# Cross-attention and expert layer of a gated Flamingo block: two heads on two partition halves instead of stacked copies of K and Q

## The reference

```python
xn = layernorm(x)
q1, k1, v1 = xn @ Wq1, xn @ Wk1, xn @ Wv1           # 8 heads of 64
k2, v2 = ctx @ Wk2, ctx @ Wv2
k, v = concat([k1, k2]), concat([v1, v2])            # 768 keys
out = softmax(q1 @ k.T / 8) @ v                      # for each batch and head
x = x + tanh(g_xattn) * (out @ Wo + bo)
xf = layernorm(x)                                    # then a mixture of experts
combine = softmax over the 2 largest of (xf @ gate_w + gate_b), 0 for the rest
y = sum_e combine[:, e] * (gelu(xf @ w1[e] + b1[e]) @ w2[e] + b2[e])   # 8 experts of 512
x = x + tanh(g_ffn) * (y + gelu(xf @ ws1 + bs1) @ ws2 + bs2)           # a shared ninth
```

## Time and profile before

| | us |
|---|---|
| median of 3 runs (172.03 to 174.6) | 172.52 |
| the profiled execution's own time | 172.02 |
| its span, first to last instruction | 169.7 |
| PE busy | 139.7 |
| DVE busy | 131.2 |
| POOL busy | 126.8 |
| ACT busy | 109.6 |
| share of the chain that ended last: PE, DVE, POOL, ACT, DMA and SP's queue | 32%, 28%, 10%, 9%, 14% |

### The profile page before, as it was taken

One profiled execution on the slowest core, in us unless ns is written; L12 is line 12 of the kernel. 1 busy time (PEld: TensorE's weight loads), 2 busy tenths in 40 slices (PEclk: granted clock), 3 DMA queues, 4 the chain that ended last, 5 costly groups with the idle time before them and its releaser, 6 DMA issues.

```text
span 169.7 us, 4332 instructions
## 1 busy us (share of the span) xinstructions
PE 139.7 (82%) x1724; PEld 111.5 (66%) x1724; DVE 131.2 (77%) x255; ACT 109.6 (65%) x182; POOL 126.8 (75%) x90
## 2 busy tenths in 40 slices
PE   7789588558699989999998892979866995999953
PEld 4435234335478768787787792869856994999952
DVE  1779999667667868768869689989999889454691
ACT  3369583329969979899968998569523462555600
POOL 7609999919999999989777955596557585868750
PEclk9999999999999999999999999999996999999999
DMA  4598699990004800995000000340000000100000
GB/s 136 184 315 211 196 238 242 220 251 14 6 0 85 198 1 16 217 233 191 4 4 0 4 0 0 108 144 6 2 0 0 4 0 4 31 0 4 0 0 31
DMA packets 12925, 13.99 MB, mean 82 GB/s; under 512 B 1470, under 2 KB 9579, under 8 KB 12907
## 3 DMA queue, kind: packets, MB, share of 16 engines
q1 hardware_dynamic: 12906, 13.73, 30.4%
HBM read 7.18 MB, written 0.26 MB: 44 GB/s over the span
## 4 chain that ended last, share of the span: by engine, by line
PE 32%; DVE 28%; POOL 10%; ACT 9%; DMA 8%; SPq 6%; issue 5%; DVEq 0%; ACTq 0%
PE banks L906 5%; DVE kab L852 5%; PE banks L908 5%; PE banks L907 5%; POOL kab L549 4%; ACT kab L642 4%; DVE v_lo L720 3%; DMA kab<-k_nat 3%; DVE nmax L735 3%; PE banks L1006 3%; PE banks L1007 3%; PE banks L987 3%; DMA ring<-in_L_ffn_w_dram 3%; SPq L425 2%; DVE gtop L763 2%
## 5 line engine op out<-in xcount | busy, mean ns | idle before, releaser
L549 POOL TENSOR_TENSOR kab<-kab 128x1024 f16<-128x1024 f32 (+1 forms) x18 | 41.1, 2283 | 17.3 <-DVE kab L852 17.3
L521 POOL TENSOR_TENSOR p_lo<-prob,p_hi 128x768 f16<-128x768 f32 x31 | 50.3, 1642 | 3.1 <-ACT p_hi L606 2.6
L642 ACT ACTIVATE kab<-banks,b1T 128x256 f32<-128x256 f32 x72 | 28.2, 478 | 24.3 <-PE banks L908 15.9
L735 DVE TENSOR_REDUCE nmax<-banks 128x1 f32<-128x768 f32 x32 | 30.5, 954 | 12.5 <-PE banks L988 12.5
L598 ACT ACTIVATE prob<-banks 128x768 f32<-128x768 f32 x32 | 25.8, 805 | 9.1 <-PE banks L1007 8.1
L906 PE MATMUL banks<-wf,kab 128*128 128x128 f16 x144 | 26.2, 224 | 5.8 <-POOL kab L549 4.5
L606 ACT ACTIVATE p_hi<-prob 128x768 f16<-128x768 f32 x32 | 27.0, 843 | 1.0
L852 DVE CAST kab<-kab 128x1024 f16<-128x1024 f32 (+1 forms) x19 | 19.5, 1031 | 9.8 <-ACT kab L642 9.8
L908 PE MATMUL banks<-wf,kab 128*128 128x128 f16 x144 | 26.2, 224 | 0.0
L907 PE MATMUL banks<-wf,kab 128*128 128x128 f16 x144 | 26.2, 224 | 0.0
L1006 PE MATMUL banks<-qab,kab 128*128 128x256 f16 x96 | 23.0, 273 | 0.7 <-DVE qab L832 0.7
(11 more groups left out here) (144 smaller groups left out, 340.3 us busy)
## 6 DMA issues: line engine op xcount, KB each, us to landing
ring<-in_L_ffn_w_dram SPq DMA_DIRECT2D x16, 256.0 KB, 4.1
kab<-k_nat SPq DMA_DIRECT2D x4, 384.0 KB, 4.4
kab<-k_nat SPq DMA_DIRECT2D x6, 192.0 KB, 4.4
kab<-k_nat SPq DMA_DIRECT2D x2, 576.0 KB, 7.2
qab<-qo SPq DMA_DIRECT2D x2, 384.0 KB, 6.2
kab<-k_nat SPq DMA_DIRECT2D x2, 288.0 KB, 7.8
prob<-in_ctx_dram SPq DMA_DIRECT2D x2, 256.0 KB, 5.4
ring<-in_L_xattn_Wk_dram SPq DMA_DIRECT2D x2, 256.0 KB, 3.9
```

The costliest lines, as they stand in the source:

```text
L521: nc.gpsimd.tensor_tensor(p_lo[:, j % 3, dst, :], prob(j, g)[:, 0:n, :], p_hi[:, j % 3, dst, :], ALU.subtract).then_inc(pl_done, 1)
L549: nc.gpsimd.tensor_tensor(hid_lo[:, k % HB, cols], hid[:, k % 2, cols], hid_hi[:, k % HB, cols], ALU.subtract).then_inc(hl_done, 1)
L642: nc.scalar.activation(hid[:, k % 2, c * T1:(c + 1) * T1], span(2 * (k % 2), HC * T1)[:, c * T1:(c + 1) * T1], ACT.Gelu, bias=b1T[:, e * H ...
L735: nc.vector.tensor_reduce(nmax[:, i, q:q + 1], span(0, KEYS), AX_X, ALU.max, negate=True).then_inc(max_done, 1)
```

## The change

The stacking copies, `kab` and `qab` are gone. Matmuls read the two heads of a pair where the projections left them, partitions 0 to 63 and 64 to 127, and the two heads' matmuls alternate, each into a PSUM bank of its own. With 64 rows a score tile needs four matmuls for each head (high·high, low·high, high·low, shift) in place of two; the shift is a product of a constant row block and a tile that DVE writes over all partitions.

The unit is now two heads by two key tiles (128x1024), three units a pair, 24 in all (NU). Maxima are taken in three chunks a pair of 128x1024, then reduced once more. Only four items precede the steps. The others lie in the dictionary `LATE`, from step -4 to step 10. Each step of PE: `shift_row`, `scores(i)`, `max_chunk`, expert work, `values`, items, tail. The scores have one PSUM buffer up to unit 12 and two from unit 13. There are 3 buffers of exponentials and 7 of their halves. `ring` has 7 places, and its loads wait for no attention step. POOL does the splits of experts 1 and 2, the bias and WO between the units. The tails begin at steps 16 and 27, the experts at FFN0 = 24.

```diff
-RING = 4
+RING = 7
+KT2 = 2
+UPP = KT // KT2
+NPAIR = B * PAIRS
+NU = NPAIR * UPP
+RINGP = 7
+RINGE = 3
+CHUNK0 = -(UPP + 1)
+DOUBLE0 = 13
+FFN0 = NU
-TAIL0 = [HEADS + PV_LAG, NH + PV_LAG + 1]
+TAIL0 = [16, 27]
-FSPLIT0 = 15
+FSPLIT0 = FFN0 - EARLY
+def chunk_of(s):
+    p, c = divmod(s - CHUNK0, UPP)
+    return (p, c) if 0 <= p < NPAIR else None
+def shift_of(s):
+    p, r = divmod(s + 1, UPP)
+    return p if r == 0 and 0 <= p < NPAIR else None
+def values_of(s):
+    if s >= NU + 1:
+        return NH - 2 + s - (NU + 1) if s <= NU + 2 else None
+    p, r = divmod(s - (UPP + 2), UPP)
+    return 2 * p + r if p >= 0 and r < 2 and p < NPAIR - 1 else None
+PRE = [(("tc", 0), 0), (("tx", 0), 2), (("k", 0, 0), 4), (("q", 0), 6)]
+LATE = {
+    -4: [(("k", 0, 1), 2)],
+    -3: [(("q", 1), 7)],
+    -2: [(("v", 0, 0), 6), (("v", 0, 1), 4)],
+    -1: [(("v", 0, 2), 5)],
+    0: [(("k", 0, 2), 4), (("q", 2), 7)],
+    1: [(("v", 0, 3), 6), (("v", 0, 4), 7)],
...
+    10: [(("v", 1, 4), 7), (("v", 1, 5), 4)],
+}
+def score_buf(u):
+    return 0 if u < DOUBLE0 else (u - DOUBLE0 + 1) % 2
@@ gpsimd
+            for i in range(STEPS):
+                if 0 <= i - 1 < LO_LAST:
+                    prob_lo(i - 1)
+                if i == 2:
+                    early_hi(1)
+                if i == 3:
+                    early_scaled(1)
+                if i == 4:
+                    early_lo(1)
+                if i == 5:
+                    add_bias()
+                if i == 6:
+                    early_hi(2)
+                if i == 7:
+                    early_scaled(2)
+                if i == 8:
+                    early_lo(2)
+                if i == 10:
+                    split_by_pool(WO)
@@ scalar
+            def exp_unit(u):
+                act.wait_ge(score_ps, u + 1)
+                if u >= RINGE:
+                    act.wait_ge(pl_done, u - RINGE + 1)
...
+                if 0 <= i < NU:
+                    exp_unit(i)
+                for n in items[0:1]:
+                    item_of(n)
+                if 0 <= i < NU:
+                    make_hi(i)
+                for n in items[1:]:
+                    item_of(n)
...
-                    if k >= 2:
+                    if k < 2:
+                        act.wait_ge(pl_done, NU - 2 + k)
+                    else:
@@ vector
+            def part_max(p, c):
+                dve.wait_ge(max_ps, UPP * p + c + 1)
...
+                nc.vector.tensor_reduce(dst, src, AX_X, ALU.max).then_inc(part_done, 1)
+            def whole_max(p):
...
+            def shift_out(p):
+                dve.wait_ge(shift_ps, p + 1)
...
@@ tensor
+            def max_chunk(p, c):
...
+                if c == 0:
+                    pe.wait_ge(item_hi, items_ready(("k", b, pp), ("q", pp)))
+                    if p == 0:
+                        read_out(before(NI, [0, 1]))
+                    else:
+                        pe.wait_ge(shift_done, p)
+                else:
+                    pe.wait_ge(part_done, UPP * p + c)
...
+            def scores(u):
...
+                for n in range(KT2):
...
+                    for half in range(2):
+                        nc.tensor.matmul(dst[:, half, cols], k_of(p, half, 0, keys), q_of(p, half, 0, every),
+                                         start=True, stop=False)
+                    for half in range(2):
+                        nc.tensor.matmul(dst[:, half, cols], k_of(p, half, 1, keys), q_of(p, half, 0, every),
+                                         start=False, stop=False)
+                    for half in range(2):
+                        nc.tensor.matmul(dst[:, half, cols], k_of(p, half, 0, keys), q_of(p, half, 1, every),
+                                         start=False, stop=False)
...
+                    for half in range(2):
+                        rows = slice(DH * half, DH * half + DH)
+                        last = nc.tensor.matmul(dst[:, half, cols], ones_row[rows, :], shift[rows, p % 2, :],
+                                                start=False, stop=True)
```

562 lines of the change are left out of this document (236 added, 326 removed), and 8 rows, old and new, of the table LATE.

## The result

| | before | after |
|---|---|---|
| median, us | 173.56 (172.03 to 174.76, 4 runs) | 187.49 (184.69 to 188.35, 4 runs) |
| profiled execution, us | 172.02 | 188.35 |
| its span, us | 169.7 | 186.6 |

The ratio is 1.0736, its 95% interval 1.0486 to 1.0985. By the medians the kernel is slower by 14 us; the prediction had it 3 us faster. Executions of one kernel differ here by 3 to 6 us: the ratios compare the shorter ones of either kernel, and the profiled execution of the kernel after is the longest of its four.

What follows compares the result with a forecast made beforehand. POOL was taken to set the pace of attention. From the profiled 172.02 us, 1.1 came off for an earlier last low half and 1.5 in the experts, giving 169.4 us; range 163.5 to 177.

Steps and rivals of the forecast that it cites:

- The lead-in: Before attention: with the stacking copies gone, first exponential at 24 us against 37.8, POOL's first low half at 27.2 against 43.76.
- The 64-row matmuls: PE's scores and maxima: alternating pairs on disjoint partitions run beside each other, 0.12 us a pair (bounds 0.11 to 0.22).
- The slow rival: 64-row matmuls run one by one, 0.22 us a pair, and PE is the bound from step 0: 180.3 us, chance 0.16.
- The price of POOL's work: POOL in attention: 23 low halves of 1024 at 2.13 us plus splits, bias and powers, sum 68.75 us.
- Can the others keep it busy?: Attention: POOL clearly slowest up to step 10 (39 us against ACT's 35); 2 us of pauses, last low half at 98.0.
- The lockstep rival: PE's in-order waits pass between engines; a late attention unit costs 2.6 us, not 2.25, over 13 units: 174 us, chance 0.17.
- The switches of rows: PE changing between 64 and 128 rows, 48 times: 0 to 0.16 us each, taken as 0.05, inside the 2 us of pauses.
- gelu 0 starts 2.0 us after POOL's last low half: Start of the experts: PE waits for the combination weights, so gelu 0 follows by 2.0 us, where it was 1.2 before.
- The experts: From attention's end to the end of the span: same work, 0 to 3.4 us gained together, 1.5 taken.
- The prediction's first step: Kernel before: POOL, with 50.3 us of work in 55.4 us, sets the pace of attention.

Runs made afterwards that it cites:

- halves apart: The changed kernel with the four score matmuls of one head first, then the four of the other: 187.34 us, profiled execution 182.73 us.
- tail two steps later: The changed kernel with the tail of batch 0 two steps later (TAIL0[0] 18 in place of 16): 181.68 us, ratio 1.0452.
- maxima and tail: The changed kernel with a pair's maxima and shift one step sooner and the tail of batch 0 two steps later: 175.97 us.
- the division ahead of the items: DVE divides a head before the items' low halves: in every step of the changed kernel, 189.26 us; only in steps with items, in the three moves, 172.55 us.
- the three moves: The changed kernel with maxima a step sooner, batch 0's tail two steps later, and DVE's division before low halves in steps with items: 172.55 us, ratio 0.9946.
- the kernel kept warm: The changed kernel with matmuls on zeros into an unread bank in three of PE's long waits: 184.82 us, profiled execution 183.56 us.

## Why the prediction was wrong, by its steps

First the sum, as the prediction cut it, against two profiled executions:

| us | forecast | after | halves apart |
|---|---|---|---|
| start to first low half | 27.2 | 29.0 | 27.3 |
| first low half to end of the last | 70.8 | 84.9 | 84.4 |
| from there to the end | 71.4 | 74.4 | 71.0 |
| sum | 169.4 | 188.35 | 182.73 |

In the shorter execution the middle line holds the whole error, 13.6 us; in the longer one 14.1 of 19.

**The lead-in: right, a little late.** Forecast 24 and 27.2; measured 25.9 and 29.04 in the profiled execution, 23.9 and 27.3 in that of "halves apart". The second is the forecast to 0.1 us; in the first PE waited 3.45 us for the first shift, against 1.93 in the second, and its next matmuls started 0.21 us apart in place of 0.11. The one term outside its bounds was the split of WV1, taken at 1.3 us (0.7 to 1.9): 2.25 and 1.68.

**The 64-row matmuls: right.** 0.12 a pair forecast, 0.11 measured. The slow rival's price of 10.9 us was near the 12 measured where the overlap was taken away, but by luck in part: it came from PE's sum as the bound of every unit, and the cost fell in two stages only.

**The price of POOL's work: right.** 2130 ns for the low half of 1024, and 67.1 us of POOL's work from the first low half to the last, where 68.75 was summed up.

**"Can the others keep it busy?": this step failed.** It said "Up to step 10 POOL is clearly slowest", from the sums of POOL (39 us) and ACT (35), and took 2 us of pauses for the rest. Measured: the pauses of POOL between its first and last low half are 113.95 - 29.04 = 84.9 less 69 of work, 16 us (15 in "halves apart"). With 10 us of POOL's work taken away the exponentials start where they did. The step compared sums of engines; what sets the pace is the lap of a loop through several of them. Three were found, each with an edit of the schedule alone:
- the maxima of a pair to its first scores: 1.8, 3.3 and 1.4 us in the three stages, in sum 6.5 (from "tail two steps later" to "maxima and tail"; by itself the edit gained 11.5, but that counts the third of this list in);
- values to division to values, with a projection between: 2.4 to 2.7 us (stage 2, with the division ahead of the items);
- the second layernorm inside attention, with xn beside POOL: 5.6 us of stage 4 (tail two steps later), 5.2 when POOL stands for it. This one and the first overlap in stage 4: both together leave 13.5 us of 20.5.

In sum, from "halves apart" to the three moves, the 71.5 us from exponential 4 to 23 become 55.8.

All was on the page of before, but for one thing: before, two units of a head had buffers of their own in PSUM and in the exponentials, and the maxima ran two steps ahead of the scores. The change took that slack, and the forecast counted it at nothing. (That the slack lay in the buffers is argued and not shown: no kernel with more of them was run.) The lockstep rival named the right mechanism ("a queue on PE with waits for maxima, shift, power and low halves, each passed on") and gave it 4.5 us, by multiplying 0.35 us by 13 units instead of following one wait once round. Followed, had the terms: a reduction of a 1024 chunk (954 for 768, so 1.27; it took 1.22), its successor, a transpose, 416 for the shift, and no values at that step on PE to lie beside it.

**The switches of rows: small.** From a 128-row projection to the scores of 64 rows it is 51.12 to 51.43, 0.31 us, where the next 512-column matmul comes after 0.22: 0.09 a switch, against 0.05 taken, and about 0.1 in the other direction too. Behind the transpose of the maxima it is more: 0.26 us from its start to the scores (67.76 to 68.02), where two transposes and no switch take 0.23 (111.19 to 111.42 in the kernel kept warm), so some 0.15 a switch. By 0.09 the 48 switches make 4.3 us of PE's time; how much of it lies where PE waits anyway was not tried. The rule of the Trainium skill, TensorEngine Tiling (Array Packing), "Key Properties", that a change of tiling mode drains the engine, shows here as 0.09 to 0.15 us a change. Its other half, that different tiles run in parallel, agrees with the pairs 0.11 apart.

**"gelu 0 starts 2.0 us after POOL's last low half": mis-sized.** 4.2 measured. The order of events was right (PE waits for the combination weights), but two of DVE's gate instructions take 1.67 (a copy of 4 columns) and 1.89 us beside POOL, PE waits 3.24, and then runs the first hidden product at the lower of its levels:

```profile
114.89 0.58 PE L1113 MATMUL banks<-ident,comb 128*9 128x128 f32 x2 [3.24 <-DVE comb_s L780]
115.27 0.42 PE L906 MATMUL banks<-x2h,wf 128*128 128x256 f16 x1
115.48 0.42 PE L907 MATMUL banks<-x2h,wf 128*128 128x256 f16 x1
```

The starts are 0.21 apart, not 0.11. In "halves apart", which makes the same instructions here, the copy took 0.96 and the other 0.16 us, the starts were 0.11 apart, and gelu followed 1.1 us after the last low half. So this term lies between 1 and 4 us from one execution to another, and makes 3.1 of the 5.6 us between these two. The 2.0 forecast lies between them.

**The experts: right in one execution, 3 us off in the other.** The prediction counted from POOL's last low half, 72.9 us before, and took 1.5 off. It is 71.0 in "halves apart", 1.9 gained, and 74.4 in the kernel after, 1.5 lost, all of it in the late first gelu: from that on either gains, "halves apart" 1.8 us and the kernel after 1.5.

## What to carry to other kernels

When buffers are merged or a unit is made larger, don't stop at the engines' sums: follow every loop through the in-order programs once round, add the latencies of a lap, and compare it with the time of a step. A busy share of 95% shows no bound; take work off that engine and see whether anything upstream starts sooner. (The prediction's first step, that POOL set the pace of the kernel before, rests on such a share and was not tried.) Two of the three loops here were cured by giving them a step or two more in the schedule, the third by setting the awaited result ahead of work that itself waits, and only in the steps where nothing more urgent stands behind it.

## What the runs showed of the hardware that was not expected

- Two matmuls on disjoint 64-row halves overlap fully even when the program gives four of one half and then four of the other: 16 matmuls in 0.88 us either way.
- A DVE instruction of 2 or 16 columns, with nothing in PSUM, can be held for about one POOL instruction: 2.08 and 2.11 us for what takes 0.16 or 0.17 undisturbed. A wait of POOL's that lets one such instruction pass gave it back at the next.
- PE waited 3 to 4 us and was granted the 1.2 GHz level afterwards (starts 0.21 apart in place of 0.11). An execution with the clock at 0.991 was no shorter (183.56 us) than one at 0.961 (182.73).
- Two executions of one kernel took 735.45 and 296.89 us at a granted clock of 1.0. In the first, the one with a profile, the matmuls were several times as long, PE 724.8 us busy, and all the other engines near their usual sums. No cause was found, and the same kernel took 182.65 to 187.89 us in its four other executions.
